# Attention phase: the output projection's statistics two heads behind their product in VectorE's order, the normalisation and the next tile's query turns one head later

## The chip, the cores and the metric

The kernel runs on one core of one Trainium2 chip. The metric is the time of one execution on the device in microseconds (us). Five engines work through queues of their own, each strictly in its order, and wait for each other on semaphores: TensorE (PE in the rows; PEld is its weight load), VectorE (DVE), ScalarE (ACT), GpSimd (POOL) and SyncE (SP), which issues transfers.

## The reference, cut to what matters

The model is one block: attention with a relative position bias, a delta rule mixer, and two mixtures of experts. The change lies in the attention, which computes, for 8 sequences of 512 positions and 16 heads of 64:

```python
xn = ln(x, g_norm)
q = l2norm(xn @ Wq) * q_scale;  kv = xn @ Wkv;  k = l2norm(k) * k_scale      # one k and v for all heads
sim = q @ k.T * 8.0 + rel_pos_bias;  sim = where(causal or masked, -max, sim)  # with one null key
out = softmax(sim) @ v
return ln(out @ Wout, g_out)      # the statistics, and the normalisation, that the change moves
```

## The kernel before, in words

**Tiles.** The queries are worked through in 32 tiles of 128 positions (4 a sequence), and each tile in 16 heads. Being causal, tile T of a sequence sees 128, 256, 384 or 512 keys, T modulo 4 telling which. "Head n" counts on over all tiles: n = 16 T + h.

**One head.** TensorE makes the scores (L455, two matmuls, called S here). VectorE adds the bias and finds the negative row maximum in one fused pass (L697). ScalarE takes the exponential (L874). TensorE turns the probabilities (L465) two heads behind, ScalarE or, for every fourth head, VectorE copies them out of PSUM (L883, L708), and four heads behind TensorE multiplies with v (L478). GpSimd adds the mask to the bias (L968) five heads ahead.

**What stands between the heads.** `order` (L275) writes one list of steps for all engines: each head, and behind it the steps that belong there. Every engine goes through the same list and does its own part of each step, so the list is each engine's queue order. `BACK` (L273) says behind which head of tile T a step for the finished tile T-1 stands: `oT` turns the output, `outp` projects it (TensorE L582, 16 matmuls, and L583), takes its mean and variance (VectorE L783 to L785) and the reciprocal root (GpSimd L1028), `hn` normalises it (L790), `hT` turns it (L588) and ScalarE copies it out (L940), and SyncE stores it. `FRONT` (L271) does the same for tiles to come: for tile T+2 `stat` (-5, so behind head 11), `xn` (-3, behind 13) and `xT` (-2, behind 14) normalise and turn the input; for tile T+1 `q0` to `kv` project it, `qs0` and `qs1` split the queries into two parts (ScalarE L916, GpSimd L1022), and `qT0` to `qT3` turn four heads each (TensorE L556), copied out by ScalarE (`qT0`, `qT2`, L920) and VectorE (`qT1`, `qT3`, L740). Steps behind the same head stand in this order: `diff0` or `weigh0` of tile T, `BACK`'s, then `FRONT`'s for T+1 and those for T+2. `weigh0` (L601) is four VectorE instructions that scale the first eight heads' output.

**Two banks for all of them.** These steps write to two PSUM banks, F0 and F1. `FILLS` (L300) says which: `xT`, `q1`, `qT0`, `qT2`, `kT` and `outp` use F0; `q0`, `kv`, `qT1`, `qT3`, `pnT` and `hT` use F1. `fill` (L430) makes TensorE wait until the bank's fill before has been read; `drained` (L310) says by whom: for `outp` it is `hn`, for `qT0` and `qT2` ScalarE's copy, for `qT1` and `qT3` VectorE's.

**What a new tile needs.** Ahead of head 0 of a tile TensorE waits for all four copies of its turned queries (L447, L448).

Of the kernel before, what the change touches and what calls it, by code (L numbers as in the profile page):

```python
# [143 lines left out]
def attention_phase(nc, a, ident, delta, mixture, hT_out, bias_rows, hT_dram, inv_dram):  # L144
# [6 lines left out]
    with ExitStack() as ctx:  # L151
# [45 lines left out]
        with ExitStack() as over:  # L197
            def mlp(name, shape):
# [19 lines left out]
        oT = sb("oT", [P, QT, P])  # L218
        hT = sb("hT", [P, TT, KD, P])
# [13 lines left out]
        hn = sb("hn", [P, D])  # L233
# [35 lines left out]


        FRONT = {"stat": -5, "xn": -3, "xT": -2, "q0": 0, "q1": 1, "kv": 2, "ss": 3, "qn": 4, "kT": 7,  # L271
                 "null": 10, "qs0": 8, "qs1": 9, "qT0": 12, "qT1": 12, "qT2": 13, "qT3": 14}
        BACK = {"diff1": 0, "weigh1": 4, "oT": 6, "pnT": 7, "outp": 9, "hn": 11, "hT": 13}  # L273

        def order():  # L275
            behind = {}
            for t in range(NT + 1):
# [3 lines left out]
                if t > 0:  # L281
                    for n, h in BACK.items():
                        behind.setdefault(NH * t + h, []).append((n, t - 1))
# [65 lines left out]
        def split_part(n):  # L349

            return (slice(None), n // 3, slice(n % 3 * D, (n % 3 + 1) * D))
# [3 lines left out]
        with nc.Block() as block:  # L355
# [236 lines left out]
            def _(dve):  # L592
# [28 lines left out]
                for name, t in steps:  # L621
# [115 lines left out]
                    elif name in ("qT1", "qT3"):  # L737
                        f = filled(name, t)
                        i = int(name[2])
                        dve.tensor_copy(qT[:, t % 2, 4 * i:4 * i + 4].rearrange("p a n -> p (a n)"), f[:, :])\  # L740
                           .then_inc(s["qT_dve"], 1)
                    elif name == "kT":
                        f = filled(name, t)
                        if t == 0:
                            dve.wait_ge(rest_in, 16 * N_REST)
                            link(dve.tensor_scalar(kscale[:, 2:3], kscale[:, 0:1], kscale[:, 1:2], SCALE,
                                                   ALU.mult, ALU.mult))
                        high, low = (kT[t // TT % 2][i][:, t % TT * P:(t % TT + 1) * P] for i in range(2))
                        if t > 0:
                            dve.wait_ge(s["kT_ready"], t)  # L750
                        dve.tensor_scalar(kf[:], f[:, 0:P], kscale[:, 2:3], None, ALU.mult).then_inc(s["kT_read"], 1)
                        dve.wait_ge(s["kT_read"], t + 1)
                        link(dve.tensor_copy(high, kf[:]))
                        dve.tensor_tensor(low, kf[:], high.bitcast(F32), ALU.subtract).then_inc(s["kT_ready"], 1)
                    elif name == "null":

                        dve.wait_ge(s["rr_ready"], t + 1)
                        link(dve.tensor_tensor(nsn[:, t % 2], nraw[:], rr[:, 0:NH], ALU.mult))
                        dve.scalar_tensor_tensor(out=nsn[:, t % 2], in0=nsn[:, t % 2], scalar=-1.0, in1=nullb[:],
                                                 op0=ALU.mult, op1=ALU.subtract).then_inc(s["null_ready"], 1)  # L760
                    elif name in ("diff0", "diff1"):
                        i, c = int(name[4]), t % 2
                        hs = slice(8 * i, 8 * i + 8)
                        dve.wait_ge(s["scores_ready"], NH * t + 8 * (i + 1))
                        dve.tensor_tensor(dn[:, i], nm[:, c, hs], nsn[:, c, hs],
                                          ALU.subtract).then_inc(s["null_diff"], 1)
                    elif name in ("weigh0", "weigh1"):
                        weigh(t, int(name[5]))
                    elif name == "oT":
                        f = filled("oT", t, 1)  # L770
                        if t > 0:
                            dve.wait_ge(full[0], filling["outp", t - 1, 0])
                        dve.tensor_copy(oT[:, 4:8].rearrange("p a n -> p (a n)"), f[:, :]).then_inc(s["oT_dve"], 1)
                    elif name == "pnT":
                        f = filled(name, t)
                        if t > 0:
                            dve.wait_ge(full[0], filling["outp", t - 1, 0])
                        dve.tensor_copy(pnrT[:], f[:, 0:P]).then_inc(s["pnrT_ready"], 1)
                    elif name == "outp":
                        f = filled("outp", t)  # L780
                        if t > 0:
                            dve.wait_ge(s["hn_ready"], t)
                        link(dve.bn_stats(stats2[:], f[:, 0:D]))  # L783
                        link(dve.bn_aggr(mv2[:], stats2[:]))
                        dve.tensor_scalar(ve2[:], mv2[:, 1:2], 1e-5, None, ALU.add).then_inc(s["out_var"], 1)  # L785
                    elif name == "hn":
                        dve.wait_ge(s["out_rstd"], t + 1)
                        if t > 0:
                            dve.wait_ge(full[1], filling["hT", t - 1, 1])
                        dve.tensor_scalar(hn[:], FB[0][:, 0:D], mv2[:, 0:1], rstd2[:], ALU.subtract,  # L790
                                          ALU.mult).then_inc(s["hn_ready"], 1)
                        if 4 * TT <= t < 4 * TT + N_SPLITS:
                            part = split_part(t - 4 * TT)
                            dve.wait_ge(delta["high_ready"], t - 4 * TT + 1)
                            dve.tensor_tensor(delta["w_low"][part], delta["wqkv"][part], delta["w_high"][part].bitcast(F32),
                                              ALU.subtract).then_inc(delta["low_ready"], 1)
# [152 lines left out]
            def _(pool):  # L949
# [25 lines left out]
                for name, t in steps:  # L975
# [14 lines left out]
                    elif name == "narrow":  # L990
                        for n in range(BM_LEAD):
                            masked_bias(n)
                    elif name == "stat":
                        pool.wait_ge(s["x_var"], t + 1)
                        pool.tensor_tensor(rstd[:], ve[:], half[:, 0:1], ALU.pow).then_inc(s["x_rstd"], 1)
                    elif name == "ss":
                        pool.wait_ge(s["ss_ready"], t + 1)
                        if t > 0:
                            pool.wait_ge(s["qn_ready"], 2 * t)
                            pool.wait_ge(s["null_ready"], t)  # L1000
                        pool.tensor_tensor(rr[:], ss[:], half[:, 0:NH + 1], ALU.pow).then_inc(s["rr_ready"], 1)  # L1001
                    elif name == "qn":
                        pool.wait_ge(s["rr_ready"], t + 1)
                        pool.wait_ge(s["q_ready"], 2 * (t + 1))
                        pool.wait_ge(s["kv_ready"], 3 * (t + 1))
                        if t > 0:
                            pool.wait_ge(full[0], filling["kT", t - 1, 0])
                        pool.tensor_tensor(kn[:], qraw[:, NH].unsqueeze(1).broadcast_to([P, 2, DH]),
                                           rr[:, NH:NH + 1].unsqueeze(2).broadcast_to([P, 2, DH]),
                                           ALU.mult).then_inc(s["kn_ready"], 1)  # L1010
                        for i in range(2):
                            hs = slice(8 * i, 8 * i + 8)
                            pool.tensor_tensor(qn[:, hs], qraw[:, hs], rr[:, hs].unsqueeze(2).broadcast_to([P, 8, DH]),
                                               ALU.mult).then_inc(s["qn_ready"], 1)
                    elif name in ("qs0", "qs1"):

                        i = int(name[2])
                        hs = slice(8 * i, 8 * i + 8)
                        pool.wait_ge(s["q_high"], 2 * t + 1 + i)
                        if t > 0:  # L1020
                            pool.wait_ge(full[1], filling["qT3", t - 1, 1])
                        pool.tensor_tensor(qs[:, hs, 1], qn[:, hs], qs[:, hs, 0].bitcast(F32),  # L1022
                                           ALU.subtract).then_inc(s["q_low"], 1)
                    elif name == "outp":
                        pool.wait_ge(s["out_var"], t + 1)
                        if t > 0:
                            pool.wait_ge(s["hn_ready"], t)
                        pool.tensor_tensor(rstd2[:], ve2[:], half[:, 0:1], ALU.pow).then_inc(s["out_rstd"], 1)  # L1028
# [1685 lines left out]
```

## Time and profile before

| | us |
|---|---|
| three runs: lowest, median, highest | 2558.45, 2561.74, 2563.37 |
| span of the profiled execution | 2563.2 |
| TensorE busy in the span | 2394.0 (93%) |
| VectorE busy | 1753.9 (68%) |
| ScalarE busy | 1234.0 (48%) |
| GpSimd busy | 1333.1 (52%) |

The profile gives the profiled execution's span; its own time is not listed apart, and the slowest run is 0.2 us above the span. The attention phase takes the time from some 55 us to 1100 us of the span, the delta rule follows, and the mixtures begin at about 1480 us. The shares are means over phases with different limits, so the rows below are taken from the attention phase, and most from single tiles in it. Tile T=10 starts at 373.8 us, T=11 at 407.5 us, T=12 at 446.1 us.

### The profile page before, as it was taken

What the parts mean: (1) busy time and instruction counts of PE and PEld (TensorE: products, weight loads), DVE (VectorE), ACT (ScalarE), POOL (GpSimd) and SP (SyncE); (2) the same over time, 40 slices, a digit from 0 to 9 for tenths busy, and PEclk for the clock granted to TensorE, in tenths of its full rate; (3) what the DMA queues carried; (4) which work ended last, traced back from release to release, by engine and by line L of the source; (5) the groups of instructions that cost most, each with busy time, mean ns of one, the idle gap of its engine ahead of it and who ended that gap; (6) DMA issues with size and microseconds to landing.
All of it is one profiled execution on the core that took longest, in us unless ns stands there. A gap on an engine that the chain in (4) does not pass through costs nothing. (4 is left out here: it accounts for less than half of the span.)

```text
span 2563.2 us, 56453 instructions
## 1 busy us (share of the span) xinstructions
PE 2394.0 (93%) x20705; PEld 1977.5 (77%) x20705; DVE 1753.9 (68%) x4121; ACT 1234.0 (48%) x3133; POOL 1333.1 (52%) x1464
## 2 busy tenths in 40 slices
PE   5999999999999999977999999988899999999998
PEld 3788888888888888845777777766677877778776
DVE  4576767677767676677888888337865755746764
ACT  3656666666666666554555555114333333332332
POOL 3676767676767676535666666215422322322332
PEclk8999999999999999988999999999999999999999
DMA  4000100000000000001122221216022112111211
GB/s 143 7 11 9 46 18 11 10 10 9 11 10 9 10 5 5 5 15 24 40 56 55 55 53 47 55 59 181 32 66 63 55 58 67 58 47 62 66 34 59
DMA packets 156689, 105.05 MB, mean 41 GB/s; under 512 B 85168, under 2 KB 134832, under 8 KB 156416
## 3 DMA queue, kind: packets, MB, share of 16 engines
q1 hardware_dynamic: 130928, 62.69, 9.0%
q10 hardware_dynamic: 25488, 38.73, 4.9%
q8 instruction: 169, 2.77, 0.4%
q14 instruction: 104, 0.85, 0.1%
HBM read 80.51 MB, written 20.88 MB: 40 GB/s over the span
## 5 line engine op out<-in xcount | busy, mean ns | idle before, releaser
L968 POOL TENSOR_TENSOR a_bm<-a_bias,a_mask_add 128x512 f32<-128x512 f32 (+3 forms) x512 | 438.4, 873 | 189.3 <-DVE a_nm L697 186.3
L1592 POOL TENSOR_TENSOR m_hid_part<-m_hid,m_hid_part 128x512 fp32r<-128x512 f32 x176 | 238.5, 1355 | 552.9 <-ACT m_hid_part L1501 547.6
L874 ACT ACTIVATE a_S<-a_S,a_nm 128x512 f32<-128x512 f32 (+3 forms) x512 | 289.3, 565 | 347.6 <-DVE a_nm L697 344.9
L697 DVE CUSTOM_DVE_ANT_0 a_S<-a_S,a_bm,a_nsn 128x512 f32<-128x512 f32 (+3 forms) x512 | 275.3, 545 | 142.1 <-PE a_S L455 137.4
L478 PE MATMUL a_O<-a_v,a_PT 128*128 128x64 f32 x2560 | 342.4, 265 | 0.0
L478 PEld LDWEIGHTS a_O<-a_v,a_PT 128*128 128x128 f32 x2560 | 328.4, 193 | 0.0
L1513 ACT ACTIVATE m_hid<-m_G 128x512 f32<-128x512 f32 x176 | 105.4, 599 | 390.9 <-PE m_G L1447 353.3
L455 PE MATMUL a_S<-a_kT,a_qT 128*128 128x384 f32 (+3 forms) x1024 | 284.0, 358 | 3.6 <-DVE a_nm L697 3.2
L1674 DVE TENSOR_TENSOR m_hid<-m_hid,m_U 128x512 f32<-128x512 f32 x176 | 121.0, 687 | 223.8 <-PE m_U L1447 190.3
L1464 PE MATMUL m_Y<-m_hid_part,m_down_high 128*128 128x512 f32 x704 | 256.5, 405 | 12.2 <-POOL m_hid_part L1592 11.4
L1447 PE MATMUL m_G<-m_in,m_gate_high 128*128 128x512 f32 x704 | 252.2, 399 | 0.9 <-POOL m_up_low L1586 0.9
L1447 PE MATMUL m_U<-m_in,m_up_high 128*128 128x512 f32 x704 | 250.7, 396 | 1.5 <-DVE m_hid L1674 1.4
L465 PE MATMUL a_T<-s_ident,a_S 128*128 128x128 f32 x1280 | 227.0, 275 | 12.2 <-ACT a_PT L883 11.3
L465 PEld LDWEIGHTS a_T<-s_ident,a_S 128*128 128x128 f32 x1280 | 160.3, 140 | 42.2 <-ACT a_S L874 15.7
L455 PEld LDWEIGHTS a_S<-a_kT,a_qT 128*128 128x128 f32 x1024 | 163.8, 192 | 18.5 <-DVE a_nm L697 6.6
L1464 PEld LDWEIGHTS m_Y<-m_hid_part,m_down_high 128*128 128x128 f32 x704 | 132.8, 189 | 47.4 <-issue 18.0
L1447 PEld LDWEIGHTS m_U<-m_in,m_up_high 128*128 128x128 f32 x704 | 132.7, 188 | 35.0 <-DVE m_hid L1674 3.0
L1447 PEld LDWEIGHTS m_G<-m_in,m_gate_high 128*128 128x128 f32 x704 | 133.3, 189 | 33.9 <-POOL m_up_low L1586 1.4
L883 ACT COPY a_PT<-a_T 128x128 f32<-128x128 f32 (+3 forms) x384 | 156.2, 407 | 0.0
L1447 PE MATMUL m_G<-m_in,m_gate_low 128*128 128x512 f32 x352 | 140.6, 399 | 0.0
L1001 POOL TENSOR_TENSOR a_rr<-a_ss,a_half 128x17 f32<-128x17 f32 x32 | 98.5, 3077 | 79.8 <-DVE a_ss L736 79.8
L1464 PE MATMUL m_Y<-m_hid_part,m_down_low 128*128 128x512 f32 x352 | 139.4, 396 | 0.0
(323 smaller groups left out, 5348.4 us busy)
## 6 DMA issues: line engine op xcount, KB each, us to landing
m_spread<-s_w ACTq DMA_DIRECT2D x64, 256.0 KB, 3.2
m_spread<-s_w ACTq DMA_DIRECT2D x128, 128.0 KB, 2.9
a_x<-in_x SPq DMA_DIRECT2D x32, 128.0 KB, 2.2
s_hT<-a_hT SPq DMA_DIRECT2D x32, 128.0 KB, 2.1
d_x<-in_x SPq DMA_DIRECT2D x8, 512.0 KB, 4.7
d_h<-s_hT SPq DMA_DIRECT2D x8, 512.0 KB, 5.2
s_xg<-d_xg SPq DMA_DIRECT2D x8, 512.0 KB, 3.1
d_x<-s_xg SPq DMA_DIRECT2D x8, 512.0 KB, 4.6
```

Of the source, the lines that this page charges most:

```text
L455: last = pe.matmul(o_s[:, 0:w], qT[:, tile % 2, h], kT[tile // TT % 2][i][:, 0:w], start=i == 0, stop=i == 1)
L465: last = pe.transpose(TB[n % 2][:, j * P:(j + 1) * P], S[:, n % S_SLOTS, j * P:(j + 1) * P], ident[:])
L478: last = pe.matmul(OB[h // 8][:, (h % 8) * DH:(h % 8 + 1) * DH], PT[:, n % PT_SLOTS, j * P:(j + 1) * P], v[tile // TT % 2][:, j], start=j ...
L697: dve.tensor_tensor_reduce(S[:, n % S_SLOTS, 0:w], SB[n % 2][:, 0:w], bm[:, n % BM_SLOTS, 0:w], -1.0, nsn[:, tile % 2, h:h + 1], ALU.add, ...
L874: act.activation(S[:, n % S_SLOTS, 0:w], S[:, n % S_SLOTS, 0:w], ACT.Exp, scale=-1.0, bias=nm[:, tile % 2, h:h + 1], accum_out=den[:, tile ...
L883: act.copy(PT[:, n % PT_SLOTS, 0:w], TB[n % 2][:, 0:w]).then_inc(s["probsT_act"], 1)
L968: pool.tensor_tensor(bm[:, n % BM_SLOTS, 0:w], bias[:, h, L - w:L], mask_add[b % 2][:, 0:w], ALU.add).then_inc(s["bm_ready"], 1)
L1447: last = pe.matmul(dst[q % 2][:, :], wts[m][j][:, k, item], x[i][:, k], start=(i, j, k) == TERMS[0], stop=(i, j, k) == TERMS[-1])
L1464: last = pe.matmul(YB[k][:, :], down[m][j][:, item, k * P:(k + 1) * P], hid_part[i][:, q % H_SLOTS], start=item == 0 and i + j == 0, stop= ...
L1513: act.activation(hid[:, q % G_SLOTS], GB[q % 2][:, :], (ACT.Copy, ACT.Silu)[ITEMS[q][1]]).then_inc(gate_active, 1)
L1592: pool.tensor_tensor(hid_part[1][:, q % H_SLOTS], hid[:, q % G_SLOTS], hid_part[0][:, q % H_SLOTS].bitcast(F32), ALU.subtract).then_inc(hi ...
L1674: dve.tensor_tensor(h, h, UB[q % 2][:, :], ALU.mult).then_inc(mult_up, 1)
```

## The change

The step `outp` is split. TensorE's part, the product, stays behind head 9. VectorE's three instructions of statistics and GpSimd's power of them become a step `ostat` of their own behind head 11. `hn` goes from head 11 to 12 and `hT` from 13 to 14, on all engines that have a part in them. The four turns of the next tile's queries, with their copies, go one head later: `qT0` and `qT1` from 12 to 13, `qT2` from 13 to 14, `qT3` from 14 to 15. `xn` stays at 13 and `xT` at 14. Which bank a step uses, and the order of the fills in each bank, stay. No instruction is added or taken away.

```diff
         FRONT = {"stat": -5, "xn": -3, "xT": -2, "q0": 0, "q1": 1, "kv": 2, "ss": 3, "qn": 4, "kT": 7,
-                 "null": 10, "qs0": 8, "qs1": 9, "qT0": 12, "qT1": 12, "qT2": 13, "qT3": 14}
-        BACK = {"diff1": 0, "weigh1": 4, "oT": 6, "pnT": 7, "outp": 9, "hn": 11, "hT": 13}
+                 "null": 10, "qs0": 8, "qs1": 9, "qT0": 13, "qT1": 13, "qT2": 14, "qT3": 15}
+        BACK = {"diff1": 0, "weigh1": 4, "oT": 6, "pnT": 7, "outp": 9, "ostat": 11, "hn": 12, "hT": 14}
...
-                    elif name == "outp":
+                    elif name == "ostat":
                         f = filled("outp", t)
                         if t > 0:
                             dve.wait_ge(s["hn_ready"], t)
...
-                    elif name == "outp":
+                    elif name == "ostat":
                         pool.wait_ge(s["out_var"], t + 1)
                         if t > 0:
                             pool.wait_ge(s["hn_ready"], t)
```

## Rows read from the trace of the kernel before

**Rows 1.** Waits of TensorE, 90 to 1085 us: waiter, releaser: us in total, times, longest.
```profile
PE a_F L556 <- DVE a_hn L790: 11.6, 16, 0.9
...
PE a_F L528 <- DVE a_xn L720: 10.9, 20, 0.6
PE a_F L556 <- ACT a_qT L920: 7.8, 24, 0.6
```

**Rows 2.** Busy times by stretch, two halves of T=10: us, then each engine; clock, DMA.
```profile
373.80:395.10 21.30, 21.21 (x150) 19.62 (x149) 13.73 (x38) 14.57 (x44) 16.31 (x16) 1.00 0.02 6
395.10:407.50 12.40, 10.54 (x87) 9.77 (x86) 11.62 (x28) 6.48 (x20) 9.88 (x10) 1.00 0.08 23
```

**Rows 3.** Waits of VectorE, 90 to 1085 us.
```profile
DVE a_stats L783 <- PE a_F L583: 89.6, 31, 3.9
```

**Rows 4.** Timeline of VectorE in T=10: start us, us, engine, line, operation, operands.
```profile
395.13 0.43 DVE L783 BATCH_NORM_STATS2 a_stats<-a_F 128x6 f32<-128x256 f32 x1 [2.86 <-PE a_F L583]
...
395.97 0.62 DVE L697 CUSTOM_DVE_ANT_0 a_S<-a_S,a_bm,a_nsn 128x384 f32<-128x384 f32 x1
...
396.59 1.28 DVE L758 TENSOR_TENSOR a_nsn<-a_nraw,a_rr 128x16 f32<-128x16 f32 x1
...
398.76 0.60 DVE L697 CUSTOM_DVE_ANT_0 a_S<-a_S,a_bm,a_nsn 128x384 f32<-128x384 f32 x1
...
405.78 0.61 DVE L697 CUSTOM_DVE_ANT_0 a_S<-a_S,a_bm,a_nsn 128x384 f32<-128x384 f32 x1
```

**Rows 5.** Timeline of TensorE in T=10: S(10), `qT2`, `xT`, and S of the next tile.
```profile
394.75 0.70 PE L455 MATMUL a_S<-a_kT,a_qT 128*128 128x384 f32 x2
...
402.93 0.63 PE L556 MATMUL a_F<-s_ident,a_qs 128*128 128x128 f32 x4 [0.36 <-ACT a_qT L920]
...
405.91 0.44 PE L528 MATMUL a_F<-s_ident,a_xn 128*128 128x128 f32 x2 [0.62 <-DVE a_xn L720]
...
407.46 0.71 PE L455 MATMUL a_S<-a_kT,a_qT 128*128 128x512 f32 x2
```

**Rows 6.** Timeline of ScalarE in T=10.
```profile
402.20 0.59 ACT L920 CAST a_qT<-a_F 128x512 fp32r<-128x512 f32 x1
...
403.29 0.62 ACT L940 ACTIVATE a_hT<-a_F,a_go 128x128 f32<-128x128 f32 x2
403.79 0.59 ACT L920 CAST a_qT<-a_F 128x512 fp32r<-128x512 f32 x1
406.43 0.62 ACT L874 ACTIVATE a_S<-a_S,a_nm 128x384 f32<-128x384 f32 x1 [2.04 <-DVE a_nm L697]
...
407.40 0.37 ACT L889 CAST a_xnT<-a_F 128x256 fp32r<-128x256 f32 x1
```

**Rows 7.** Timeline of GpSimd in T=10: bias, power of `outp`, split of queries.
```profile
394.70 1.00 POOL L968 TENSOR_TENSOR a_bm<-a_bias,a_mask_add 128x384 f32<-128x384 f32 x1
396.05 0.55 POOL L1028 TENSOR_TENSOR a_rstd<-a_ve,a_half 128x1 f32<-128x1 f32 x1 [0.34 <-DVE a_ve L785]
396.57 1.27 POOL L1022 TENSOR_TENSOR a_qs<-a_qn,a_qs 128x512 fp32r<-128x512 f32 x1
```

**Rows 8.** Timelines of VectorE, TensorE and ScalarE at the end of T=12.
```profile
471.88 0.34 DVE L697 CUSTOM_DVE_ANT_0 a_S<-a_S,a_bm,a_nsn 128x128 f32<-128x128 f32 x1
...
472.01 0.44 PE L528 MATMUL a_F<-s_ident,a_xn 128*128 128x128 f32 x2 [0.38 <-DVE a_xn L720]
...
472.93 0.47 PE L455 MATMUL a_S<-a_kT,a_qT 128*128 128x256 f32 x2
...
472.26 0.40 ACT L874 ACTIVATE a_S<-a_S,a_nm 128x128 f32<-128x128 f32 x1 [0.86 <-DVE a_nm L697]
...
472.81 0.37 ACT L889 CAST a_xnT<-a_F 128x256 fp32r<-128x256 f32 x1
```

**Rows 9.** Timelines of VectorE and TensorE at the end of T=11.
```profile
442.76 0.74 DVE L697 CUSTOM_DVE_ANT_0 a_S<-a_S,a_bm,a_nsn 128x512 f32<-128x512 f32 x1
...
446.08 0.42 PE L455 MATMUL a_S<-a_kT,a_qT 128*128 128x128 f32 x2
```

## The prediction

> **What bounds the kernel now.** Read first the waits of TensorE in the attention phase [rows 1]: TensorE works through its queue in order, and in some 1000 us it stands still for few. The three rows add up to 30.3 us, and all lie at steps 12 to 14 of a query tile: for the normalised rows `hn`, for the next tile's `xn`, and for ScalarE's copy of turned queries. Then the busy shares of the two halves of one tile, the tile T=10 (384 wide) [rows 2]: up to the end of the output projection TensorE is busy 21.21 of 21.30 us and VectorE only 13.73; from there to the end of the tile VectorE is busy 11.62 of 12.40 us (94%), TensorE 10.54 (85%). So TensorE sets the first stretch, and in the second both are nearly full, and bound to each other. Last VectorE's waits [rows 3]: 89.6 us go by ahead of the 31 `bn_stats` of the output projection, 2.9 us each. The reader should ask what VectorE could do in them.
>
> I call the score product of head h S(h), VectorE's fused score pass (L697) R(h), so R(14) is what head 14's exponential waits for.
>
> **Part 1: the statistics from 9 to 11.** They wait for a product that TensorE makes in 3.9 us behind head 9. With them gone from step 9, R(10) stands there. But S(10) is behind the same product in TensorE's queue, so R(10) can't start before it either: S(10) starts at 394.75 and ends at 395.45 [rows 5], and R(10) starts today at 395.97 [rows 4]. VectorE's long wait changes its name, from L783 to L697, and gets 0.5 us shorter at its end, as R(10) starts at some 395.49. Against this the three statistics instructions, 395.13 to 395.97, 0.84 us [rows 4], ran mostly beside S(10), where VectorE had nothing else; they now follow R(11), in the stretch where VectorE has 6% to spare. Net at R(14): 0.84 - 0.48 = +0.36 us a tile.
>
> GpSimd's power for `rstd2` moves with them. It took 0.55 us and held GpSimd waiting from 395.70 to 396.05 [rows 7]; `qs1` now starts at 395.70 instead of 396.57. The power is late for nothing: `hn` comes a head behind the statistics, with the next tile's statistics and R(12) between, over 1.3 us of VectorE's time.
>
> What the earlier `qs1` does to VectorE is the uncertain term. Today the 16 column `nsn` product starts at 396.59 and lasts 1.28 us, to the end of `qs1` (396.57 to 397.84) [rows 4, 7], though it has only 16 columns to do. With `qs1` from 395.70 to 396.97 and the bias of head 15 behind it to 397.97, the small operations at step 10 are held until then and R(11) starts at 398.0 instead of 398.76, 0.76 earlier. The same sort of hold at `weigh0` may cost more; I give 0.2. So R(14) starts at 398.0 + (405.78 - 398.76) + 0.84 + 0.2 = 406.06, +0.3 us. In other tiles it may be a microsecond more or less (both ends kept: -1.2 to +1.3 a tile), since a hold there today may be missing, or come new.
> [...]
>
> **Part 2: `hn`, the query turns and `hT` one head later.** The time of the operations stays; what changes is the order and who waits.
>
> (a) `hn` behind R(12), `qT0` behind S(13). `qT0` writes bank F0, which holds the projection until `hn` has read it. Both move by one head, so this wait (11.6 us in all [rows 1]) stays about as it is.
>
> (b) `xT` right behind `qT2`. At step 14 TensorE's queue now reads `hT`, `qT2`, `xT`. `qT2` and `xT` use the same bank F0 (`FILLS`, L300), and `fill` lets `xT` start only when ScalarE has copied `qT2` out. Before, `qT2` stood at step 13, and a whole head and `qT3` lay between. That copy is now in ScalarE's queue at step 14 too: behind the exponential of head 14, the copy of head 12's turned probabilities and the two operations of `hT`. The exponential waits for R(14), which in VectorE's queue stands behind everything of step 13: `weigh0`, the `qT1` copy and `xn`. So TensorE gets to `xT` and waits for this path [rows 4 to 6]: R(14), 0.61 us; exponential and copy, 406.43 to 407.40, 0.97; `hT`, 403.29 to 403.79, 0.50; the `qT2` copy, 0.59; and the two hand-overs, 0.04 (R(14) lasts from 405.78 to 406.39, the exponential starts at 406.43) and 0.14 (ScalarE's `qT0` copy lasts from 402.20 to 402.79, TensorE's `qT2`, which waits for it, starts at 402.93). The sum is 2.85 us from R(14)'s start: `xT` at 406.06 + 2.85 = 408.91 instead of 405.91 [rows 5], 3.0 later.
>
> (c) `qT3` at step 15, the last before the next tile. S(16) needs all of its queries (L447, L448). After `xT` TensorE does head 15 (405.91 to 407.46, 1.55 with `xT` itself [rows 5]), then `qT3`, 0.63 like `qT2` [rows 5], VectorE's copy of it 0.69 (an estimate: 0.1 above the 0.59 of ScalarE's copy of this shape), and the hand-overs 0.04 and 0.14 again: 1.50, of which TensorE stands still for 0.87. S(16) starts at 408.91 + 1.55 + 1.50 = 411.96 instead of 407.46: **+4.5 us for T=10**.
>
> (d) TensorE's share of this. The waits before are inside the difference, since I compare S(16) with S(16). What could hide them is other work of TensorE behind `hT`, but its queue is in order and has only `qT2` there, 0.63 us, which itself comes before the copy waited for. SP's and GpSimd's queues: only the `hT` store moves, by one head, and nobody waits for it for four tiles.
>
> The other widths by the same path. T=12 (128 wide) [rows 8]: R(14) 471.88 + 0.3; 0.34 for R; exponential and copy 472.26 to 472.81, 0.55; 1.27 for `hT`, `qT2` and hand-overs: `xT` at 474.34; then 472.01 to 472.93, 0.92, and 1.50: S(16) at 476.76 instead of 472.93, +3.8. T=11 (512 wide) [rows 9]: R(14) 442.76 + 0.3; 0.74; the exponential with copy 1.18 and the last head with `xT` 1.87 (estimates, carried on in equal steps from the 128 and 384 wide tiles); 1.27; 1.50: S(16) at 449.62 instead of 446.08, +3.5. There TensorE was the slower one before, which hides more. For 256 wide I take 4.2, between its neighbours. Mean 4.0.
>
> **The sum.** Nothing gives this back: in heads 0 to 9 of the next tile TensorE is the bound (99.6% busy in [rows 2]), so a later S(16) moves all behind it. The full pattern occurs in T=1 to 29, 29 tiles: 29 x 4.0 = 116 us. In T=0 there is no `hn` and `hT` but the `qT2`, `xT` and `qT3` part: 3 us. In T=30 there is no `xT`, only `qT3`: 1.3 us (0.87 and some of the shift of R(14)). Together 120 us. The profiled execution has a span of 2563.2 us, nearly all of a run's time (its slowest run is 2563.37), and is 1.5 us above the median of 2561.74. So 2563.2 + 120 = 2683, 2682 us against the median.
>
> **The rivals.**
> - *A, forecast:* the path above, 2682 us. For it: the order of the queues is written out, and each duration is a row. Chance 0.80.
> - *B, only the bare new waits:* if R(14) came so early that ScalarE were done when TensorE arrives, only the `qT2` turn and copy (0.63 + 0.59 + 0.18) and the `qT3` turn and copy (1.50) would show, 2.9 us a tile, and the waits of [rows 1] (1.0 us a tile) would be gone: +1.9 x 30 = 57, 2620 us. Against it: VectorE's 94% [rows 2]. Chance 0.06.
> - *C, the gain:* the turns a head later find `hn`, `xn` and the copies done, and the waits of [rows 1] go, with nothing new: 2563 - 30 = 2533 us. It decides at `xT`: only if the bank F0 were free when TensorE gets there. For it: 30.3 us are waited there today. Against it: (b). Chance 0.05.
> - *D, no change:* VectorE's wait only changes its name, and the new waits take the place of the old ones: 2562. Chance 0.03.
> - *E, worse:* the holds by GpSimd fall badly in every tile (+1.3 instead of +0.3, 30 us), or the granted clock, 1.00 in both stretches [rows 2], falls as TensorE goes from 85% to some 62% busy (10.54 of 16.9 us) in the second: a tenth of 10.5 us in 30 tiles, another 32. 2712 us or more. Chance 0.06.
>
> **How the numbers follow.** The predicted time is A's, 2682. Its own bounds are those of the hold: -1.2 instead of +0.3 takes 44 us off, but not in all tiles at once, as T=10 was worked out; three quarters of it, 33, gives 2649; +1.3 gives 2712. I put the range at 2645 to 2712, which leaves out B, C and D. About 0.2% (5 us) is what a measurement of this kernel can tell from no change. Faster 0.05 (C), same 0.03 (D), slower 0.92 (A, B, E).
>
> **What would show it.** In the trace after: at L783 no wait to speak of, and at L697 some 90 us more of waiting for S; `xT` (L528) waiting some 2 us a tile for ScalarE's `qT` copy (L920); a new wait of S (L455) for VectorE's copy (L740), 0.7 us a tile; `hT` (L588) waiting longer for L740; TensorE busy time unchanged; from 1480 us on everything the same, shifted. It would be wrong if `xT` doesn't wait for L920, or if tiles were to last as long as before.

## The result, and the profile after

Over four runs the changed kernel takes 2790.36 us in the median (2778.98 to 2803.76), the one before 2562.18 us (2558.45 to 2563.37): ratio 1.0894, 95% interval 1.0857 to 1.0930, slower by 228 us. The direction was forecast, the size not: I had said 2682 us and at most 2712. The profiled execution has a span of 2801.8 us, 238.6 more than the profiled one before; its own time is 2803.76.

First the tiles T=3 to 30, 28 of them, as one stretch: length, then busy time of TensorE, its weight load, VectorE, ScalarE and GpSimd, the granted clock, and DMA. Before:

```profile
152.90:1046.20 893.30, 841.16 (x6105) 765.12 (x6104) 636.99 (x1851) 554.23 (x1743) 634.22 (x679) 1.00 0.04 12
```

And after:

```profile
175.10:1280.30 1105.20, 963.11 (x6103) 865.75 (x6103) 644.21 (x1849) 566.22 (x1741) 635.30 (x678) 0.87 0.04 10
```

The stretch is 211.9 us longer. TensorE stands still for 142.1 us of it instead of 52.1, which is 90.0 us of the loss. The other 121.9 us are in its busy time, for the same matmuls, while the clock was granted at 0.87 instead of 1.00. The first three tiles are another 22 us longer, and all that follows on T=30 only some 5 us.

TensorE's waits after, as in [rows 1] (90 to 1350 us):

```profile
PE a_F L528 <- ACT a_qT L920: 48.8, 29, 2.8
PE a_F L588 <- DVE a_qT L740: 25.7, 24, 2.3
PE a_S L455 <- issue: 25.1, 30, 0.9
...
PE a_F L556 <- DVE a_hn L790: 14.6, 22, 1.4
```

`xT` (L528) waits no more for `xn` but for ScalarE's copy of `qT2`; `hT` (L588) waits for VectorE's copy of `qT1`, 25.7 us where it was 5.2 before; and 30 times the first scores of a tile stand behind a wait that the profile calls "issue" and that spans VectorE's `qT3` copy. VectorE's 89.6 us at L783 [rows 3] are gone from its waits, and those at L697 have grown from 124.8 us (90 to 1330 us here, 90 to 1085 before):

```profile
DVE a_S L697 <- PE a_S L455: 325.7, 161, 4.9
DVE a_xnT L727 <- ACT a_xnT L889: 96.8, 30, 3.7
```

Now T=10, which was worked out ahead, in five stretches (compare [rows 2]; the product ends at 469.25 here, at 395.09 before):

```profile
447.90:469.30 21.40, 21.22 (x148) 19.65 (x149) 12.48 (x35) 13.49 (x39) 15.00 (x14) 1.00 0.00 1
469.30:478.00 8.70, 7.12 (x56) 6.43 (x55) 8.19 (x20) 4.23 (x13) 7.09 (x8) 1.00 0.01 3
478.00:482.00 4.00, 1.89 (x16) 1.66 (x13) 3.71 (x8) 0.38 (x2) 1.84 (x3) 0.93 0.00 0
482.00:494.00 12.00, 9.41 (x36) 7.93 (x35) 2.49 (x7) 4.61 (x14) 3.67 (x3) 0.50 0.07 22
494.00:500.00 6.00, 6.00 (x39) 5.19 (x38) 1.99 (x5) 4.00 (x9) 2.28 (x2) 0.91 0.01 3
```

Up to the product nothing has changed. From 478 to 482 us TensorE is busy for 1.89 of 4.00 us, and for the next 12 us its clock is 0.50, where it was 1.00 up to 478. In shorter stretches the clock is 1.00 up to 481.25 us, 0.80 in the next quarter of a microsecond, and 0.50 from 481.50 to 495.0. Its timeline there (start, length, operation; compare [rows 5]):

```profile
476.59 1.07 PE L556 MATMUL a_F<-s_ident,a_qs 128*128 128x128 f32 x8 [0.35 <-DVE a_hn L790]
...
478.18 0.78 PE L478 MATMUL a_O<-a_v,a_PT 128*128 128x64 f32 x6
481.07 0.41 PE L588 MATMUL a_F<-s_ident,a_hn 128*128 128x128 f32 x2 [2.11 <-DVE a_qT L740]
481.31 0.96 PE L556 MATMUL a_F<-s_ident,a_qs 128*128 128x128 f32 x4
484.03 0.66 PE L528 MATMUL a_F<-s_ident,a_xn 128*128 128x128 f32 x2 [1.75 <-ACT a_qT L920]
484.34 0.99 PE L455 MATMUL a_S<-a_kT,a_qT 128*128 128x384 f32 x2
485.13 0.84 PE L465 MATMUL a_T<-s_ident,a_S 128*128 128x128 f32 x3
485.76 1.38 PE L478 MATMUL a_O<-a_v,a_PT 128*128 128x64 f32 x6
486.93 1.06 PE L556 MATMUL a_F<-s_ident,a_qs 128*128 128x128 f32 x4
488.82 1.20 PE L455 MATMUL a_S<-a_kT,a_qT 128*128 128x512 f32 x2 [0.83 <-issue]
```

`hT` starts at 481.07 after 2.11 us of standing still, `xT` after another 1.75, and S(16) after 0.83. The clock falls just after `hT`'s start, so after the first of the three. From `qT2` on every group lasts longer: 0.96 where [rows 5] had 0.63. And ScalarE's and VectorE's side of it, the path of part 2 (b) and the operations of step 10 (compare [rows 4, 6]); first ScalarE:

```profile
481.81 0.61 ACT L874 ACTIVATE a_S<-a_S,a_nm 128x384 f32<-128x384 f32 x1 [3.62 <-DVE a_nm L697]
...
482.78 0.63 ACT L940 ACTIVATE a_hT<-a_F,a_go 128x128 f32<-128x128 f32 x2
483.29 0.59 ACT L920 CAST a_qT<-a_F 128x512 fp32r<-128x512 f32 x1
```

then VectorE:

```profile
469.64 0.62 DVE L697 CUSTOM_DVE_ANT_0 a_S<-a_S,a_bm,a_nsn 128x384 f32<-128x384 f32 x1 [3.21 <-PE a_S L455]
470.18 0.94 DVE L765 TENSOR_TENSOR a_dn<-a_nm,a_nsn 128x8 f32<-128x8 f32 x1
471.05 1.04 DVE L758 TENSOR_TENSOR a_nsn<-a_nraw,a_rr 128x16 f32<-128x16 f32 x1
472.12 1.20 DVE L759 SCALAR_TENSOR_TENSOR a_nsn<-a_nsn,a_nullb 128x16 f32<-128x16 f32 x1
473.25 0.60 DVE L697 CUSTOM_DVE_ANT_0 a_S<-a_S,a_bm,a_nsn 128x384 f32<-128x384 f32 x1
...
481.16 0.60 DVE L697 CUSTOM_DVE_ANT_0 a_S<-a_S,a_bm,a_nsn 128x384 f32<-128x384 f32 x1
...
488.03 0.69 DVE L740 CAST a_qT<-a_F 128x512 fp32r<-128x512 f32 x1 [1.95 <-PE a_F L556]
...
490.83 0.16 DVE L765 TENSOR_TENSOR a_dn<-a_nm,a_nsn 128x8 f32<-128x8 f32 x1
```

and GpSimd beside step 10:

```profile
469.81 1.29 POOL L1022 TENSOR_TENSOR a_qs<-a_qn,a_qs 128x512 fp32r<-128x512 f32 x1
471.04 2.25 POOL L968 TENSOR_TENSOR a_bm<-a_bias,a_mask_add 128x384 f32<-128x384 f32 x2
```

The three small VectorE operations from 470.18 on end at 471.12, 472.09 and 473.32, each within 0.1 us of the end of a GpSimd operation (`qs1` at 471.10, the two biases, one row here, at 472.05 and 473.29). The first of them takes 0.16 us at 490.83, where GpSimd is idle.

### The profile page after: what moved, and what is told of

Same layout as the page of the kernel before. It is cut to its first block and busy times, and to the rows that moved or that the text cites. A ratio compares the mean times of both kernels' runs of the same rounds, so it can differ in the third digit from the quotient of the medians.

```text
span 2801.8 us, 56453 instructions
## 1 busy us (share of the span) xinstructions
PE 2529.7 (90%) x20705; PEld 2089.3 (75%) x20705; DVE 1761.3 (63%) x4121; ACT 1246.3 (44%) x3133; POOL 1335.5 (48%) x1464
## 5 line engine op out<-in xcount | busy, mean ns | idle before, releaser
L697 DVE CUSTOM_DVE_ANT_0 a_S<-a_S,a_bm,a_nsn 128x512 f32<-128x512 f32 (+3 forms) x512 | 277.2, 545 | 341.7 <-PE a_S L455 338.4
L478 PE MATMUL a_O<-a_v,a_PT 128*128 128x64 f32 x2560 | 373.5, 281 | 0.0
L478 PEld LDWEIGHTS a_O<-a_v,a_PT 128*128 128x128 f32 x2560 | 363.5, 210 | 0.0
L455 PE MATMUL a_S<-a_kT,a_qT 128*128 128x384 f32 (+3 forms) x1024 | 309.5, 386 | 43.5 <-issue 25.1
L465 PE MATMUL a_T<-s_ident,a_S 128*128 128x128 f32 x1280 | 247.6, 295 | 18.9 <-ACT a_PT L883 18.0
L455 PEld LDWEIGHTS a_S<-a_kT,a_qT 128*128 128x128 f32 x1024 | 183.2, 213 | 73.1 <-issue 37.1
L465 PEld LDWEIGHTS a_T<-s_ident,a_S 128*128 128x128 f32 x1280 | 172.9, 150 | 54.9 <-ACT a_S L874 25.5
L544 PE MATMUL a_F<-a_wqkv,a_xnT 128*128 128x512 f32 (+1 forms) x576 | 161.7, 425 | 2.1 <-ACT a_bias L867 1.3
```

Source lines behind the costliest of these rows:

```text
L455: last = pe.matmul(o_s[:, 0:w], qT[:, tile % 2, h], kT[tile // TT % 2][i][:, 0:w], start=i == 0, stop=i == 1)
L465: last = pe.transpose(TB[n % 2][:, j * P:(j + 1) * P], S[:, n % S_SLOTS, j * P:(j + 1) * P], ident[:])
L478: last = pe.matmul(OB[h // 8][:, (h % 8) * DH:(h % 8 + 1) * DH], PT[:, n % PT_SLOTS, j * P:(j + 1) * P], v[tile // TT % 2][:, j], start=j ...
L544: last = pe.matmul(f[:, 0:cols.stop - cols.start], xnT[i][:, k], wqkv[j][:, k, cols], start=n == 0, stop=n == len(terms) - 1)
L697: dve.tensor_tensor_reduce(S[:, n % S_SLOTS, 0:w], SB[n % 2][:, 0:w], bm[:, n % BM_SLOTS, 0:w], -1.0, nsn[:, tile % 2, h:h + 1], ALU.add, ...
```

## The experiments

Theory 1: the loss comes from the turns' new place, by two ways. TensorE stands still at `hT`, `xT` and S(16), and the clock falls behind that. Theory 2: it comes from the moved statistics, which hold VectorE. A third reading is that the clock fell for another reason than the standstills. "Clock" below is that of T=3 to 30 in the profiled run.

**e1, part 1 alone.** The turns are back in their places.

```diff
-                 ... "qT0": 13, "qT1": 13, "qT2": 14, "qT3": 15}
-        BACK = {... "outp": 9, "ostat": 11, "hn": 12, "hT": 14}
+                 ... "qT0": 12, "qT1": 12, "qT2": 13, "qT3": 14}
+        BACK = {... "outp": 9, "ostat": 11, "hn": 12, "hT": 13}
```

> The changed kernel with its part 1 and hn alone: statistics at step 11, hn at 12, the query turns back at 12 to 14 and hT at 13. Theory 1 (the loss of 228 us comes from the turns' new place: TensorE idle at hT, xT and S(16), and the granted clock that falls behind them): only a small part, qT0 waits for the later hn, +1 to 1.5 us a tile, so 2600 us (2580 to 2640) and a mean clock of at least 0.97. Theory 2 (the statistics and their later start hold VectorE and so all): near the changed kernel, 2750 to 2790 us.

Measured: 2632.67 us, ratio 1.0276 (1.0257 to 1.0295), clock 0.95. One wait makes up most of TensorE's standing still, 90.8 us in T=3 to 30:

```profile
PE a_F L556 <- DVE a_hn L790: 83.0, 30, 3.9
```

The time is inside theory 1's range, the clock is below it (0.966 over the whole run, where at least 0.97 was expected). `qT0` needs the bank that `hn` empties, and with this one wait of 2.8 us a tile (83.0 in 30) the clock is already lower than in the kernel before. In T=3 to 30 the standing still grows by 38.7 us over the kernel before, and the busy time of the same matmuls by 23.5.

**e2, the turns alone.**

```diff
-                 ... "qT0": 12, "qT1": 12, "qT2": 13, "qT3": 14}
-        BACK = {... "outp": 9, "hn": 11, "hT": 13}
+                 ... "qT0": 13, "qT1": 13, "qT2": 14, "qT3": 15}
+        BACK = {... "outp": 9, "hn": 11, "hT": 14}
```

> The kernel before with the turns (13, 13, 14, 15) and hT (14) moved alone; statistics at 9 and hn at 11 as before. Theory 1: most of the loss, 2740 us (2700 to 2790), with the wait of xT for ScalarE's copy at some 45 us and granted clock 0.50 stretches. Theory 2: near the kernel before, 2560 to 2590 us.

Measured: 2764.49 us, ratio 1.0788 (1.0760 to 1.0816), clock 0.90. The waits are those of the whole change:

```profile
PE a_F L528 <- ACT a_qT L920: 54.3, 29, 2.5
PE a_F L588 <- DVE a_qT L740: 33.4, 23, 1.9
PE a_S L455 <- issue: 24.9, 30, 0.8
```

So the turns alone cost 202 us of a loss of 228, and theory 2 falls as the main cause. The parts don't add up (70 + 202 is more than 228): in the whole change `hn` and `qT0` move together, and most of e1's wait is gone.

**e3, the changed kernel with `xT` at 15.**

```diff
-        FRONT = {"stat": -5, "xn": -3, "xT": -2, ...
+        FRONT = {"stat": -5, "xn": -3, "xT": -1, ...
```

> The changed kernel with xT one head later (step 15), so that a head stands between qT2 and xT, which share bank F0. Theory 1: the 49 us wait of xT for ScalarE's copy goes; hT's 26 us and S(16)'s 25 us stay; with shorter standstills the clock falls less often: 2650 us (2610 to 2700). A rival in which the clock falls for another reason than these standstills: the wait goes, the clock stays near 0.93, 2740 us.

Measured: 2659.69 us, ratio 1.0385 (1.0364 to 1.0406), clock 0.96. The wait at L528 for L920 is gone from the list; at `hT` it stays:

```profile
PE a_F L588 <- DVE a_qT L740: 28.5, 22, 2.3
```

A head between `qT2` and `xT` gives back 131 of the 228 us, though only 49 us were waited there. More than the wait comes back because the clock does: in T=3 to 30 TensorE stands still 47.8 us less than in the changed kernel, and its matmuls take 80.7 us less.

**e4, the changed kernel with TensorE kept busy.** The order of the steps and what each waits for stay, and ahead of the three waits TensorE runs matmuls that nobody reads; lines are 3 to 9 higher than before.

```diff
+                                if 0 < tile < NT:
+                                    pe.wait_ge(s["scores_ready"], n - 1)
+                                    unread(3, SB[0])
                                 pe.wait_ge(s["qT_act"], 2 * (tile + 1))
...
                     elif name == "xT":
+                        if t >= 2:
+                            pe.wait_ge(s["scores_ready"], NH * (t - 2) + 14)
+                            unread((4, 7, 8, 10)[(t - 2) % TT], SB[1])
...
                     elif name == "hT":
+                        if t + 1 < NT:
+                            pe.wait_ge(s["scores_ready"], NH * (t + 1) + 14)
+                            unread((1, 3, 8, 0)[(t + 1) % TT], SB[1])
```

> The changed kernel with matmuls that nobody reads in the places where TensorE stands still (1, 3, 8, 0 ahead of hT, 4, 7, 8, 10 ahead of xT by width of the tile, 3 ahead of S(16); 512 columns of bf16 each, into score banks already read). They add work and take away none of the waits. Theory 1: the granted clock stays at 0.98 or above in the attention phase, and the time falls to 2690 us (2665 to 2720), about what the prediction gave without the clock (2682). Rival (the low clock isn't caused by TensorE standing still, or costs little): 2790 us or more.

Measured: 2705.28 us, ratio 1.0557 (1.0538 to 1.0575). T=3 to 30:

```profile
167.10:1185.70 1018.60, 945.12 (x6466) 819.40 (x6466) 643.48 (x1849) 566.41 (x1741) 635.65 (x679) 0.97 0.04 11
```

And the unread matmuls in it (167 to 1186 us: busy, mean ns, idle before):

```profile
L427 PE MATMUL a_S<-s_ident 128*128 128x512 bf16 x363 | 93.3, 387 | 0.0
```

This is the run that settles the size. More work on TensorE, some 400 matmuls more, makes the kernel 85 us faster than the changed one. The clock is at 0.97 instead of 0.87 (I had expected 0.98); 73.5 us of standing still are not filled. Without the 93.3 us of unread matmuls the kernel's own take 851.8 us, 10.7 more than before, where in the changed kernel they take 121.9 more: so 111 of those 121.9 us go when the clock stays up. What is left, 143 us over the kernel before, is near the 120 us of the prediction, which had no clock in it. It is an upper bound on the path alone, as some unread matmuls outlast the standstill that they fill: `xT` still waits in only 19 tiles, where it waited in 29.

**e5, `qT2` alone one head later**, on the kernel before.

```diff
-                 ... "qT2": 13, "qT3": 14}
+                 ... "qT2": 14, "qT3": 14}
```

> The kernel before with qT2 alone one head later (14, ahead of qT3 and xT). It isolates the shared bank F0: xT then waits for ScalarE's copy of qT2 with only qT3 between. Theory 1: a wait of xT for L920 of 1 to 1.5 us a tile in place of the 0.35 us for xn, +30 us without the clock, 2590 us; if the clock falls behind it too, up to 2640 us. Rival (xT's wait only stands where VectorE is late anyway, because of the moved statistics): 2562 us, no change.

Measured: 2655.98 us, ratio 1.0360 (1.0331 to 1.0390), clock 0.95.

```profile
PE a_F L528 <- ACT a_qT L920: 72.2, 30, 3.5
```

The move of `qT2` towards `xT`, on the bank that they share, makes 2.4 us of waiting a tile by itself, more than the 1 to 1.5 expected, and costs 92 us, more than the 2640 us that I allowed. The rival, that it needs the moved statistics, falls.

**e10, `qT3` alone at 15**, on the kernel before (`"qT3": 14` to `"qT3": 15`).

> The kernel before with qT3 alone one head later (15). Only S(16)'s wait for VectorE's copy is new, 0.87 us a tile in 31 tiles: +25 us by the prediction's part (c), 2588 us (2580 to 2600), clock unchanged at 1.00 in the attention phase. Rival (the clock falls behind any new standstill): 2620 us or more.

Measured: 2614.13 us, ratio 1.0202 (1.0185 to 1.0219), clock 1.00.

```profile
PE a_S L455 <- issue: 35.6, 30, 1.4
PE a_F L528 <- DVE a_xn L720: 20.2, 21, 1.1
```

+53 us where 25 were expected, outside the range (2580 to 2600 us), though the clock stays up. T=3 to 30:

```profile
157.00:1097.20 940.20, 846.75 (x6103) 767.63 (x6103) 627.89 (x1849) 559.12 (x1741) 634.35 (x679) 1.00 0.04 12
```

That is 46.9 us longer than before, of which 41.3 are TensorE's standing still (93.5 instead of 52.1) and 5.6 its busy time. VectorE's timeline in T=10 shows what I had left out (TensorE's `qT3` starts at 424.06, S(16) at 426.05):

```profile
424.39 0.42 DVE L727 TENSOR_TENSOR a_xnT<-a_F,a_xnT 128x256 fp32r<-128x256 f32 x1 [1.41 <-ACT a_xnT L889]
424.73 0.61 DVE L697 CUSTOM_DVE_ANT_0 a_S<-a_S,a_bm,a_nsn 128x384 f32<-128x384 f32 x1
...
425.26 0.69 DVE L740 CAST a_qT<-a_F 128x512 fp32r<-128x512 f32 x1
```

`xT`'s low part, held until ScalarE has copied the high one, and R(15) stand in VectorE's order ahead of the copy of `qT3`, so that S(16) waits 1.2 us a tile (35.6 in 30) and not the 0.87 that I had counted. And `xT` waits 20.2 us for `xn` (10.9 before), which fits that the 0.63 us of `qT3` no longer lie ahead of it on TensorE. In the changed kernel S(16) waits less (25.1 us), as `xT` itself is late there.

**e9, the changed kernel with VectorE relieved.**

```diff
-        FRONT = {"stat": -5, ... "null": 10, ...
-                    behind.setdefault(NH * t + 10, []).append(("diff0", t))
+        FRONT = {"stat": -8, ... "null": 8, ...
+                    behind.setdefault(NH * t + 9, []).append(("diff0", t))
```

> The changed kernel with VectorE relieved: the input's statistics and nsn at step 8, diff0 at step 9. R(14) should then come some 2.5 us earlier. Theory 1 with my path (R(14), ScalarE, qT2's copy, xT, qT3, S(16)): the waits at xT fall, but the turn and copy of qT2 (1.4 us) and of qT3 (1.5 us) stay bare, with fewer and shorter standstills the clock mostly stays: 2620 us (2590 to 2660). Rival (VectorE's load isn't what sets R(14)): 2780 us or more.

Measured: 2746.69 us, ratio 1.0723 (1.0706 to 1.0740), clock 0.90. Expected were 2590 to 2660 us, and by the rival 2780 or more: it is neither. The waits at `xT` and S(16) are as large as in the changed kernel:

```profile
PE a_F L528 <- ACT a_qT L920: 51.6, 29, 2.5
PE a_F L588 <- DVE a_qT L740: 33.6, 18, 2.4
PE a_F L556 <- DVE a_hn L790: 28.1, 22, 1.7
```

VectorE's timeline of T=10 has the reason:

```profile
457.18 0.54 DVE L790 TENSOR_SCALAR a_hn<-a_F,a_mv,a_rstd 128x256 f32<-128x256 f32 x1 [1.33 <-POOL a_rstd L1028]
...
458.64 1.01 DVE L607 TENSOR_TENSOR a_dent<-a_den,a_pn 128x8 f32<-128x8 f32 x1
```

`hn` now waits 1.33 us for GpSimd's power, which stands in GpSimd's queue behind two biases; in `weigh0` the first operation, on 8 columns, again takes 1.01 us beside a bias of GpSimd's (0.99 before; its median in e9's attention phase is 0.16). R(14) comes 1.7 us earlier in T=10 than in the changed kernel, where 2.5 were expected (10.2 us after the product instead of 11.9), and so does `xT` (13.1 instead of 14.8), but TensorE gets to `hT` 1.6 us earlier too (8.1 us after the product instead of 9.7), and the standstill stays. So it is less VectorE's load that makes the standstill than the order: between TensorE's arrival at `hT` and the start of `xT` the path runs through VectorE (`weigh0`, copy, `xn`, R(14)) and ScalarE whatever came before.

**e6, `xT` alone at 15**, on the kernel before (`"xT": -2` to `-1`).

> The kernel before with xT alone one head later (15). Its 10.9 us of waiting for xn go; nothing else changes unless q0 of the next tile then waits for xnT. If the waits of TensorE are what this stretch costs: 2562 - 8 = 2554 us (2548 to 2560). If q0 waits in their place: 2562 to 2572 us.

Measured: 2588.77 us, ratio 1.0102 (1.0077 to 1.0126), slower than both cases that I had written down. The wait only moves, and grows:

```profile
PE a_F L544 <- ACT a_xnT L889: 17.8, 22, 0.9
PE a_S L455 <- DVE a_qT L740: 6.9, 13, 0.6
```

**e7, the input's statistics at step 8**, on the kernel before (`"stat": -5` to `-8`).

> The kernel before with the input's statistics (stat, L713 to L715, 0.8 us of VectorE a tile) at step 8 instead of 11, so ahead of VectorE's wait for the product. If VectorE's full stretch sets heads 10 to 15 with TensorE, moving 0.8 us of its work into the 2.9 us wait takes off up to the 1.0 us a tile that TensorE waits: 2540 us (2530 to 2555). Rival, that VectorE's wait is no room since R(9) gets late and with it T(9): 2562 us or more.

Measured: 2545.80 us, ratio 0.9936 (0.9917 to 0.9955): faster, 16 to 18 us, in the range. The 0.8 us of work go into VectorE's wait at L783, which shrinks to 61.5 us in 30 tiles from 85.7 (90 to 1050 us, both), and TensorE's standing still in T=3 to 30 falls from 52.1 to 41.5 us:

```profile
150.70:1028.90 878.20, 836.67 (x6105) 765.69 (x6104) 629.23 (x1851) 554.37 (x1743) 633.93 (x679) 1.00 0.04 13
```

**e8, the small operations of step 10 too** (`"null"` to 8, `diff0` to 9).

> As the one before, and the small operations of step 10 too: nsn (L758, L759) at step 8 and diff0 (L765) at step 9. They lasted 2.25 us in T=10, most of it held by GpSimd. If the wait has room for both: all of the TensorE waits in heads 11 to 14 go, 2528 us (2520 to 2545). Rival: step 8 now holds R(9) up by more than the 2.9 us, and S(11) waits: 2562 us or more.

Measured: 2549.07 us, ratio 0.9945 (0.9929 to 0.9960). Faster than before, but no more than e7: L783 waits only 5.8 us, so the room is used up, and `xT` waits 25.3 us for `xn` (17.4 in e7). The time is just outside the range (2520 to 2545 us).

**e11, the statistics at 8 and `xn` at 12** (`"stat": -8, "xn": -4`).

> The kernel before with the input's statistics at step 8 and xn at 12. The 17.4 us that xT still waits for xn in the kernel with the statistics at 8 alone should go: 2546 - 15 = 2531 us (2525 to 2545). Rival: hT then waits longer for VectorE's copy of qT1, which comes behind xn or R(13) late, and nothing is won, 2546 us.

Measured: 2542.17 us, ratio 0.9922 (0.9910 to 0.9935), the fastest of all, and faster than both kernels. `xT`'s wait is gone; a smaller one of `qT3` for `hT`'s copy came (7.3 us). The time is inside the range, but its distance to e7, 4 us where 15 were expected, is within their spread.

**e12, the output's statistics at 10 on top of it** (`"outp": 9, "ostat": 10, "hn": 11`).

> As the one before, and the output projection's statistics at step 10, one head behind their product, hn still at 11, turns in their old places: the part of the change that gives R(10) back its 0.5 us without moving the turns. Expected no gain over the one before: hn then waits for GpSimd's power, 0.55 us behind the statistics with one score pass between; 2530 to 2545 us. If the statistics' place mattered by itself: 2520 us or less.

Measured: 2563.08 us, ratio 1.0006 (0.9991 to 1.0020), 21 us slower than e11 and outside the range (2530 to 2545 us).

```profile
PE a_F L556 <- DVE a_hn L790: 27.5, 23, 1.6
```

Moving the statistics off their product costs something even with one head: `hn` then waits for the power and `qT0` for `hn`.

## Why the prediction was right and wrong

**Part 1, VectorE's wait keeps its place.** Right. R(10) starts 0.39 us after the product's end, predicted 0.40 (395.49 less 395.09). L783 no longer waits and L697 does, though by 201 us more where I had said some 90: VectorE also waits for scores that the standstills and the clock make late.

**Part 1, the holds by GpSimd.** Under-sized. I let two GpSimd operations hold step 10 and R(11) start 2.9 us after the product. Three operations of VectorE, 0.94, 1.04 and 1.20 us for 8 and 16 columns, each ended within 0.1 us of the end of a GpSimd operation, and R(11) starts at 473.25, 4.0 us after it. R(14) starts 11.9 us after the product, predicted 11.0. This one term is 0.94 us in T=10.

**Part 2 (b), the path to `xT`.** Right, and nearly to the last tenth: from R(14) to `xT` 2.87 us (481.16 to 484.03), predicted 2.85. e5 and e3 show the cause each from its side.

**Part 2 (c), `qT3` and S(16).** The wait is there, 25.1 us in 30 tiles, 0.83 each for 0.87 predicted. That is in part luck: I hadn't looked at what stands ahead of the `qT3` copy in VectorE's order, and by itself the move makes 1.2 us (e10). But `xT` to S(16) took 4.79 us (484.03 to 488.82) instead of 3.05. TensorE's own work is longer here, not the waiting: the clock is 0.50 there. It takes S(16) to 7.2 us later than before in T=10, where 4.5 were predicted: 0.94 of the hold, and 1.74 of this.

**The step that failed is the clock: the sum has no term for it, and rival E sizes it far too small.** I had it there as a tenth of 10.5 us a tile, 32 us together, with chance 0.06. TensorE's busy time, which I had said would stay unchanged, grew by 121.9 us in 28 tiles, 4.4 us a tile, and this belongs to the forecast itself: the standstills that I predicted are what brings the clock down. I read 1.00 in [rows 2] at 85% busy and took it as a slow slope. The trace after shows two levels: of 4421 quarters of a microsecond in T=3 to 30, 3202 are at 1.00, 1159 at 0.50, and the other 60 each lie between one and the other; before, all 3574 are at 1.00. T=10 shows how it gets there: TensorE stands still for 0.66, 0.58 and 0.35 us between 473 and 477 us and for 2.11 us from 478.96, and with `hT` and `qT2` just begun the clock goes to half, ahead of the next standstill of 1.75 us. It stays there for 13.5 us, far into the next tile. The `q` projection at 491.59 takes 2.91 us for its six matmuls, the next one at 496.03 1.64. In e4 the same order of steps, with TensorE busy in its waits, cost 85 us less, at a clock of 0.97 for 0.87. In T=3 to 30 of the changed kernel no single standstill lasted over 2.8 us. How many of them, how long and how close together, make the clock fall is not shown.

**The sum.** Predicted 4.0 us a tile, 112 in 28 tiles, of the path alone. Measured, with the clock mostly kept (e4): 125.3 us in the same tiles, of which 10.7 are still the kernel's own matmuls taking longer, and part is unread matmuls that outlast the waits and the deeper holds. With the clock: 211.9. By width, 128 to 512, a tile of T=3 to 30 is in the mean 4.1, 5.3, 5.3 and 3.2 us longer than before in e4 (predicted 3.8, 4.2, 4.5 and 3.5) and 7.5, 8.4, 7.9 and 6.5 in the changed kernel. So the path, its place and its waits were right, and the time was outside the range since a second effect of those waits was left to a rival.

**The rivals.** B, C and D are out by the result. B's reasoning, that an earlier R(14) leaves only bare waits, was tried in e9 and doesn't hold there. C, the gain, exists by another way: work moved into VectorE's 2.9 us (e7, e11), not the turns moved out.

What stays open is the exact split of the 228 us between path and clock, since the longer TensorE work also moves the waits, and since e4's unread matmuls are not exactly as long as the standstills.

## What to carry to other kernels

Two steps that use the same buffer need other work between them on the engine that fills it; moving one of them next to the other was a wait of 2.4 us a tile here (e5), small as the move looks. Where VectorE waits for a product that stands ahead of its own next input in TensorE's queue, moving the waiting step won nothing here (the wait went to L697); moving independent work into the wait did (e7). And where TensorE is the bound, ask of each new standstill whether the clock falls behind it: e10's, up to 1.4 us long, cost little but their own time (5.6 us of busy time beside 41.3 of standing still), while with waits of 2.4 to 2.8 us at one place the half clock came on top, in 349 of 3822 quarters of a microsecond in e1 and 359 of 3920 in e5, and in the changed kernel it cost more than the standing still.

## What the runs showed of the hardware

- The granted clock is 1.00 in T=3 to 30 with waits of up to 1.0 us (the kernel before) and, but for 30 of 3761 quarters of a microsecond, with waits of 0.8 to 1.4 us ahead of each tile's first scores (e10). It is 0.95 with one place of 2.4 to 2.8 us a tile (e1, e5). With three places it is 0.87 where they add up to 3.3 us a tile (the change) and 0.90 where they add up to 3.8 (e2), so the sum of the waits alone doesn't order the runs.
- The same goes for all standing still in T=3 to 30: 93.5 us of it in e10 came with 5.6 us more of busy time than before, 90.8 us in e1 with 23.5.
- At 0.50 TensorE's groups in T=10 are 1.5 to 1.8 times as long: `xT` 0.66 us for 0.44, four turns 1.06 for 0.63, six products with `v` 1.38 for 0.78.
- Three VectorE operations in a row on 8 and 16 columns took 0.94, 1.04 and 1.20 us beside GpSimd's instructions; the first of them takes 0.16 us where GpSimd is idle.
